# A language-model layer on one core: front reordered, and batch 1's stage with its row of maxima sent sooner

## The reference

```
h = einsum('bsd,bsde->bse', base[ids], rule_transform[token_rules[ids]])
h = h + attention(layernorm(h))    # softmax(q k^T / 8) over 512 keys, 8 heads
h = h + experts(layernorm(h))      # top 2 of 8, relu, softmax of the two gates
```

## Time and profile before

| | |
|---|---|
| three runs | 608.01, 612.52, 615.87 us; median 612.52 |
| profiled execution | 610.8 us, its span 608.8 us, granted clock 0.93 |
| busy in the span | PE 495.7 (81%), DVE 411.8 (68%), ACT 287.2 (47%), POOL 229.1 (38%) |
| chain that ended last | PE 55%, DVE 18%, POOL 9%, issue 8%, DMA 4%, ACT 4%, SP's queue 2% |

### The profile page before, as it was taken

One profiled execution on the slowest core, in us unless ns is written; L12 is line 12 of the kernel. 1 busy time (PEld: TensorE's weight loads), 2 busy tenths in 40 slices (PEclk: granted clock), 3 DMA queues, 4 the chain that ended last, 5 costly groups with the idle time before them and its releaser, 6 DMA issues.

```text
span 608.8 us, 9495 instructions
## 1 busy us (share of the span) xinstructions
PE 495.7 (81%) x2764; PEld 270.0 (44%) x2764; DVE 411.8 (68%) x1003; ACT 287.2 (47%) x581; POOL 229.1 (38%) x375
## 2 busy tenths in 40 slices
PE   0168404878777888999999999999999999999985
PEld 0036302444442334445544544554454445576663
DVE  5634288883126756888868968986984876755477
ACT  0205101037663535465565565555566545547673
POOL 5765356462425200431352254032322313181542
PEclk9999665579998997999999999999999999999988
DMA  8825210919620171532330431134042200000000
GB/s 237 316 65 168 62 35 28 210 57 232 195 79 18 35 171 36 123 74 63 82 76 2 104 90 34 30 90 101 2 104 63 52 2 11 1 10 2 11 2 17
DMA packets 21792, 47.05 MB, mean 77 GB/s; under 512 B 6249, under 2 KB 11577, under 8 KB 21681
## 3 DMA queue, kind: packets, MB, share of 16 engines
q1 hardware_dynamic: 15408, 32.23, 21.9%
q0 software_dynamic: 4752, 8.20, 4.5%
q10 hardware_dynamic: 1584, 6.03, 3.0%
HBM read 9.97 MB, written 11.01 MB: 34 GB/s over the span
## 4 chain that ended last, share of the span: by engine, by line
PE 55%; DVE 18%; POOL 9%; issue 8%; DMA 4%; ACT 4%; SPq 2%; DVEq 0%; ACTq 0%; POOLq 0%
PE bank L1304 15%; PE bank L1290 10%; PE bank L1266 7%; POOL ctxT L522 5%; PE bank L1214 4%; PE bank L1236 4%; DVE mx L1009 4%; DMA ctxT<-in_table,ids 2%; PE bank L1208 2%; PE bank L1209 2%; DVE r_sb L1067 2%; POOL r_sb L595 2%; POOL emb_sorted L532 1%; PE bank L1315 1%; PE bank L1249 1%
## 5 line engine op out<-in xcount | busy, mean ns | idle before, releaser
L1009 DVE TENSOR_REDUCE mx<-bank 128x1 f32<-128x512 f32 x256 | 170.7, 687 | 79.0 <-PE bank L1290 72.8
L595 POOL TENSOR_TENSOR r_sb<-r_sb 128x256 f32<-128x256 f32 x174 | 90.9, 523 | 248.9 <-DVE r_sb L1085 168.5
L675 ACT ACTIVATE prob<-bank 128x512 f32<-128x512 f32 x256 | 138.8, 597 | 68.7 <-PE bank L1266 56.3
L1304 PE MATMUL bank<-prob,xa 128*64 128x512 f32 x448 | 123.5, 630 | 0.0
L1290 PE MATMUL bank<-ks,qs 96*128 96x512 f32 x240 | 111.4, 467 | 13.9 <-DVE mx L1009 13.8
L1290 PEld LDWEIGHTS bank<-ks,qs 96*128 96x128 f32 x240 | 46.2, 193 | 121.8 <-issue 103.4
L1266 PE MATMUL bank<-qs,ks 97*128 97x512 f32 x224 | 77.3, 427 | 0.0
L742 ACT ACTIVATE r_sb<-bank,stay 128x512 f32<-128x512 f32 x56 | 37.1, 687 | 44.9 <-PE bank L1209 44.6
L1266 PEld LDWEIGHTS bank<-qs,ks 97*128 97x128 f32 x224 | 38.6, 194 | 15.3 <-issue 10.5
L522 POOL DMA_INDIRECT ctxT<-in_table,ids x32 | 33.2, 1036 | 22.5 <-DMA ctxT<-in_table,ids 9.6
L532 POOL DMA_INDIRECT emb_sorted<-ctxT,pos x32 | 32.3, 1009 | 20.4 <-DMA emb_sorted<-ctxT,pos 12.2
(11 more groups left out here) (173 smaller groups left out, 696.2 us busy)
## 6 DMA issues: line engine op xcount, KB each, us to landing
qs<-qk_h SPq DMA_DIRECT2D x64, 128.0 KB, 2.5
ks<-qk_h SPq DMA_DIRECT2D x56, 128.0 KB, 2.5
qs<-qk_l SPq DMA_DIRECT2D x32, 128.0 KB, 2.5
ks<-qk_l SPq DMA_DIRECT2D x28, 128.0 KB, 2.4
emb_sorted<-front ACTq DMA_DIRECT2D x4, 608.0 KB, 9.7
y_sorted<-y_out POOLq DMA_DIRECT2D x19, 128.0 KB, 2.4
e_in<-emb_sorted POOLq DMA_DIRECT2D x9, 256.0 KB, 4.0
emb_sorted<-front ACTq DMA_DIRECT2D x3, 640.0 KB, 9.7
```

Source lines behind the costliest of these rows:

```text
L595: nc.gpsimd.tensor_tensor(a[:, at:at + width], src[:, 0:width], src[:, width:2 * width], ALU.add).then_inc(S["pool_chain"], 1)
L675: nc.scalar.activation(prob[:, step % NPROB, u % 2, :], bank[u % NST][:], ACT.Exp, scale=SC).then_inc(S["exp_done"], 1)
L1009: V.tensor_reduce(mx[:, u // 16, at_:at_ + 1], score_bank(n)[:], AX.X, ALU.max).then_inc(S["mx_done"], 1)
L1304: last = M(bank[5][64 * hh:64 * hh + 64, :], xa[:, b % XAR, ut, :], prob[:, step, hh, :], start=(ut == 0), stop=(ut == J - 1))
```

## The change

- Front, DVE: within the 15 groups only quarter 2 is looked at (after groups 5 to 8). Quarter 3's look and `starts(1)` follow the loop. PE counts quarter 3 after the last group has been evicted. The slots of quarters 1, 2 and 3 all come after the norm of batch 0, moved on at steps 1, 2, 5 (twice) and 7 of stage -2, and the rest at (-2,9); quarters 2 and 3 are one double run with one set of small operations.
- Front, POOL: the memset of `xa` goes ahead of the last 14 fetches; `values(0)` stands behind quarter 1's scatter instead of behind that of quarters 1 and 2.
- `tile_rules(1)` and `rule_row(1)` move from (-2,9) to (-1,15).
- Rule groups start at (0,2) instead of (0,3). Batch 1: norm (0,0), xT (0,2), proj (0,2) and (0,3), before (-1,12), (-1,15), (0,0) and (0,1). Batch 2: norm (0,10), xT (0,12), proj (0,13) and (0,14), before (0,11), (0,14) and (0,15). Batch 3: xT (1,8), proj (1,9) to (1,12), before (1,4) and (1,5) to (1,8). rt of batch 0: (1,8), before (1,6).
- SP: in b = 1, max_row(1,1) comes first; srow, stack(2,2) and stack(2,3) follow. stack(2,2) is no longer sent in b = 0.

```diff
-        R_AT = [(0, 3 + g // 4) for g in range(20)]
+        R_AT = [(0, 2 + g // 4) for g in range(20)]
-            return {1: (-1, 15), 2: (0, 14)}.get(nb, (nb - 2, XT))
+            return {1: (0, 2), 2: (0, 12), 3: (1, 8)}.get(nb, (nb - 2, XT))
-            return {1: ((0, 0), (0, 0), (0, 1), (0, 1)), 2: ((0, 15), (0, 15), (0, 15), (0, 15))}.get(
+            return {1: ((0, 2), (0, 2), (0, 3), (0, 3)), 2: ((0, 13), (0, 13), (0, 14), (0, 14)),
+                    3: ((1, 9), (1, 10), (1, 11), (1, 12))}.get(
                 nb, [(nb - 2, k) for k in PROJ])
-            if k == RT and 0 <= b - 1 < B:
+            if k == (RT if b != 1 else 8) and 0 <= b - 1 < B:
             for b in range(-2, B):
+                if b == 1:
+                    max_row(1, 1)
                 if 0 <= b - 1 < LAST:
 ...
+                if b == 1:
+                    stack(2, 2)
                 if 0 <= b + 1 < B:
                     stack(b + 1, 3)
-                if 0 <= b < B:
+                if 0 <= b < B and b != 1:
                     max_row(b, 1)
 ...
-                if 0 <= b + 2 < B:
+                if 0 <= b + 2 < B and b != 0:
                     stack(b + 2, 2)
 ...
             place(0, range(FIRST))
+            nc.gpsimd.memset(xa[:], 1.0).then_inc(S["xa_set"], 1)
             for c in range(FIRST + 10, NC):
 ...
-            nc.gpsimd.memset(xa[:], 1.0).then_inc(S["xa_set"], 1)
 ...
-            place(1, range(FIRST, FIRST + 2 * QC))
+            place(1, range(FIRST, FIRST + QC))
             values(0)
-            place(1, range(FIRST + 2 * QC, NC))
+            place(1, range(FIRST + QC, NC))
 ...
-            def slots(i, q):
+            def slots(i, q, parts=1):
+                c0, c1 = q * QC, (q + parts) * QC
 ...
+                for p in range(parts):
+                    at_ = c0 - lo + p * QC
+                    link(V.tensor_tensor(sel[:], oh[:, at_:at_ + QC, :], key.unsqueeze(1).to_broadcast([128, QC, NR]), ALU.mult))
+                    yield
+                    link(V.tensor_reduce(slot_f[:, p * QC:(p + 1) * QC], sel[:], AX.X, ALU.add))
+                    yield
 ...
-            later = chain(look(1, 2), look(1, 3))
+            later = look(1, 2)
 ...
-                if 5 <= g < 9 or g >= 11:
+                if 5 <= g < 9:
                     next(later, None)
-            run(later)
+            run(look(1, 3))
             starts(1)
-            run(slots(1, 1))
-            run(slots(1, 2))
 ...
-            N_AT = {1: (-1, 12), 2: (0, 11), 3: (0, 15)}
+            N_AT = {1: (0, 0), 2: (0, 10), 3: (0, 15)}
 ...
-                    later = slots(1, 3)
+                    later = chain(slots(1, 1), slots(1, 2, 2))
 ...
                     if (b, k) == (-2, 9):
                         run(later)
+                    if (b, k) == (-1, 15):
                         tile_rules(1)
-                    if b == -2 and k in (1, 2, 5, 6, 7, 8):
+                    for _ in range({1: 1, 2: 1, 5: 2, 7: 1}.get(k, 0) if b == -2 else 0):
                         next(later, None)
 ...
-                    for _ in range(4 if b == -1 else 3 if b == 0 else 3 if b == LAST else 1):
+                    for _ in range((4 if k < 3 else 3) if b == 0 else 3 if b == LAST else 1):
 ...
-                if g in (8, 11, 13):
-                    count(1, (8, 11, 13).index(g) + 1)
+                if g in (8, 11):
+                    count(1, (8, 11).index(g) + 1)
             pe.wait_ge(S["y_ok"], NG[0])
+            count(1, 3)
 ...
-                    if (b, k) == (-2, 9):
+                    if (b, k) == (-1, 15):
                         rule_row(1)
```

More of the change, by code:

```diff
@@ L170, in lm_tower_kernel @@
             trule = tb("trule", [128, 1])
-            slot_f = tb("slot_f", [128, QC])
-            slot_i = tb("slot_i", [128, 11, QC], I32)
+            slot_f = tb("slot_f", [128, 2 * QC])
+            slot_i = tb("slot_i", [128, 11, 2 * QC], I32)
         with ExitStack() as part:
@@ L529, in place @@
                         pool.wait_ge(S["scattered_1"], 16 * (c - FIRST))
-                    if c % QC == 0:
+                    if c in (0, QC, 2 * QC):
                         pool.wait_ge(S["pos_ok"], c // QC + 1)
@@ L823, in starts @@
                 link(V.scalar_tensor_tensor(key, first, float(B * T), cum, ALU.mult, ALU.add))
-            def slots(i, q):
-                c0, c1 = q * QC, (q + 1) * QC
+            def slots(i, q, parts=1):
+                c0, c1 = q * QC, (q + parts) * QC
                 lo = SPAN[i][0]
[L829 to L834, removed]
+                both, nth, ahead, at_in, past, gap, tile_, hi, mid, low, two = (slot_i[:, j, 0:c1 - c0] for j in range(11))
+                for p in range(parts):
[4 more added lines that the diff above has]
+                    yield
+                link(V.tensor_tensor(both, slot_f[:, 0:c1 - c0], rank[:, c0:c1], ALU.add))
                 link(V.tensor_scalar(nth, both, SHIFT, (B * T >> SHIFT) - 1, ALU.logical_shift_right, ALU.bitwise_and))
```

## The result

The changed kernel takes 625.62 us (median of four runs, 623.97 to 626.20) against 612.09 (four runs, 608.01 to 615.87): ratio 1.0209, interval 1.0161 to 1.0257. It is slower; whether by more than 2% the interval leaves open. The profiled execution took 623.97 us, span 622.0, against 610.8 and 608.8: 13.2 us more, where I forecast 6.05 (median 617, range 605 to 626).

A forecast was written before the change was run, and what follows sets the result against it. TensorE, 81% busy, was taken as dense except in the first third, where waits break its beat at four places. Terms -2.3 + 3.5 + 2.15 - 1.0 - 3.6 + 7.3 = +6.05 on 610.8 gave 616.9, forecast 617, range 605 to 626.

The forecast's parts named there:

- Front: Up to the first rule group: gathers and norm come sooner, rules start at 137.8 instead of 141.0, 3.2 us sooner.
- So the scatter starts where it started before: POOL's scatter: waits ten us for slots now behind the norm, starts at 90.9 and ends at 133.8, no change.
- holds two more projections (0.9): Rule section: starts 3.2 us sooner but holds two more projections costing 0.9, together -2.3 us.
- I take +3.5: Rule section: a cold start after some 8 us idle slows four groups and one step, +3.5 us, bounds 0 and 16.6.
- The extra step and the wait for the gather of batch 2: Behind the rules: same wait, one more step left behind it, +2.15 us; batch 2's projections two by two, -1.0 us.
- (1,5) to (1,12): Stage 1: the 8.3 us lost at (1,6) become 4.7, with a wait of 2.7 at (1,10): -3.6 us, bounds -5.6 to 0.
- (1,15): Stage 1: new wait of 4.5 us for the row of maxima behind two stacks, +7.3 us with clock loss, bounds +4.5 and +8.
- Rival 1: Scatter: faster for the change, first rule group at 132.6, clock kept: -2.7 us, 608 us, chance 0.2.
- Rival 2: Rule section: stays at the lower clock from start to end, 16.6 in place of 3.5: 630 us, chance 0.1.
- Rival 3: Stage 1: ACT, stopped at (1,9), also holds the exponentials; the whole 8.3 us remain: +9.7, 620.5 us, chance 0.12.
- rival 4: Stage 1: stalls at (1,6) and (1,15) both vanish and rival 1 holds: -14.7 us, 596 us, chance 0.05.
- Nothing later takes it back: Stages from b=2 on keep their beat, so a gain or loss up to there moves the end by the same amount.

The follow-up runs named there:

- experiment 5: The changed kernel unaltered, run again on another chip: 633.14 us, ratio 1.0286 to the kernel before.
- experiment 9: The kernel of experiment 1 with slot run 1 put back in front of the norm of batch 0: 603.14 us, ratio 0.9855.
- experiment 6: The changed kernel with eight extra matmuls of 384 columns, results unused, ahead of the first rule group: 632.53 us, ratio 1.0265.
- experiment 7: The changed kernel with batch 1 (norm, x, projections) back where it was, rule groups still from (0,2): 622.07 us, ratio 1.0156.
- experiment 2: The changed kernel without its stage 1 part (batch 3, SP's order and rt as before): 627.47 us, ratio 1.0227.
- experiment 4: The changed kernel with max_row(2,0) moved ahead of stack(3,0) and stack(3,1) on SP's queue: 624.42 us, ratio 1.0153.
- experiment 12: The changed kernel with the edits of experiment 4 and experiment 9, and stack(2,2) sent in b = 0: 604.56 us, ratio 0.9898.
- experiment 11: The kernel of experiment 10 with the norm of batch 2 at (0,12) instead of (0,11): 593.81 us, ratio 0.9691.
- experiment 8: The kernel of experiment 3 with the edit of experiment 4 and stack(2,2) sent in b = 0 again: 604.38 us, ratio 0.9813.
- experiment 1: The changed kernel's front alone, with rule groups, batches 1 to 3 and SP's order as in the kernel before: 618.48 us, ratio 1.0101.
- experiment 10: The edits of experiment 8 and experiment 9 together: 601.92 us, ratio 0.9802 to the kernel before.
- experiment 3: The kernel before with the change's stage 1 part alone (batch 3's xT and projections, rt, SP's order): 618.46 us, ratio 1.0102.

## Why the prediction was right or wrong

- **The result as a whole.** The time, 625.62, lies 0.4 us inside the range's end of 626 and outside the 611 to 623 that I gave my own forecast; "slower" had a chance of 0.11. In experiment 5, on another chip, all four runs of the same kernel (631.44 to 635.55) lie above the range. That the range held is in part luck.
- **Front: right, within 2.7 us.** Forecast against measured: gathers 70.8 and 69.13, norm 78 and 75.74, maxima 99.5 and 96.80, start of the scatter 90.9 and 89.13, e_in load 133.8 and 131.88, first rule group 137.8 and 135.23. "So the scatter starts where it started before" holds, and experiment 9 shows that it was the order of norm and slots that held it. The start of the gathers was right by luck: I had the loop end at 68.3 and the stores 2.5 us behind it, but it ended at 65.0, and the fetches, which I had left out, ended the wait. TensorE was idle for 4.99 us ahead of the rules, where I had some 8.
- **Rules: the step that failed is the term of the section, "holds two more projections (0.9)" and "I take +3.5".** That makes a section of 42.4 us; it took 49.2, 6.8 more (2.6 of it made good by the sooner start). By sets, the 11.2 us over the kernel before are 5.85 in the first (12.38 against 6.53), 3.1 in the second (11.76 against 8.67) and 2.25 in the third (11.19 against 8.93); the rest is as long as before.
  - The first set takes 8.60 us when it runs warm (experiment 6). So the cold start cost 3.8 us in this execution, close to the 3.5, though only 1.4 in experiment 5 and 1.8 in experiment 7. The two projections, with PE's wait of 0.94 for their qk_l, cost the other 2.1, not 0.9.
  - The 5.35 us of the second and third set I had put at nothing. I had not asked when batch 1's first stack must be there: its scores want it at (0,4), and the last projection now stands in (0,3), before in (0,1). By the chain of waits above these scores start at 156.15, 20.9 us behind the first turn; before, the tile behind the second set started 13.4 behind it. So 7.5 of the 11.2 us, the cold start among them, are set by the path from the rules' start over projections and remainder to the stack. The other 3.7 are slow clock behind it.
  - In all traces with the changed placement the stack ends a wait, 19 to 22 us after the first turn, with slow matmuls behind it: 0.73 us in the first profile, 2.89, 2.96, 1.34, 3.79 and 1.91 in experiments 2, 4, 5, 6 and 12. With batch 1 early it does so once, for 0.38 us (experiment 9).
  - In the first profile the clock had fallen just before that wait, at 153.14. What let it fall is not settled: the small waits there (0.94 for qk_l at 147.61, 0.71 and 0.85 for ACT) stand in experiment 12 too, at full clock, and in experiment 11, with no stack wait, it fell behind one of 1.05 us for ACT (an apply at 143.89 takes 1.12 us).
- **The extra step and the wait for the gather of batch 2: right.** +2.15 and -1.0 were forecast behind the section, together +1.15; measured +1.5 (from +5.4 to +6.9). The wait itself is 3.79 us, before 3.94.
- **(1,5) to (1,12): place and releaser right, size not.** The wait at (1,10) is 2.38 us where I had 2.7, ended by qk_l. The net is -1.9 instead of -3.6.
- **(1,15): right.** A wait of 5.50 us ended by the row's transfer, forecast 4.5; from (1,12) to (2,0) it costs 8.2, forecast 7.3. Experiment 4 takes it away by the queue order alone.
- **Sum.** 6.05 + 4.2 (section) + 0.35 + 1.7 + 0.9 = 13.2. Of the error of 7.15 us, 4.2 are one term.
- **The rivals.** Rival 1 (the scatter is faster) did not come: it took 42.75 us instead of 42.85. Its two long waits moved forward with the stacks, to 98.54 (3.84 us) and 106.90 (3.16). Rival 2 had the right consequence in part. The Trainium skill ("TensorE: Matmul & The Clock Gate", section "A second HAM failure mode: psum-queue depth-cycling") says that small idles between groups can keep the clock switching between its two levels. It does not say that it stays low, as rival 2 had it. The trace agrees with the switching: applies of 1.12 us up to 140.16, of 0.69 at 148 to 151, of 1.12 from 153.14 and of 0.69 from 171.16 on. The section was thus not cold from start to end, and experiment 7, with idles of 0.58 and 0.95 us between its groups at 151.90 and 153.88, stayed at 1.00. Rival 3, the whole 8.3 us staying, did not come: 1.9 were won, about half way between it and the forecast. The time of rival 4 (596) was reached by experiment 11 (593.81) alone, with two edits of order that the change lacked and with batches 1 and 2 and the rule groups where they had been.
- **What I did not know.** The 617 assumed that part 0's loop takes what it took before. In the changed kernel it ended at 65.0 in one execution and at 76.8 in another, and the time followed (medians 625.6 and 633.1). "Nothing later takes it back" also failed once, in the profiled execution of experiment 8.

## What to carry to other kernels

When a queue issues in program order and waits for a transfer to land, ask of each small transfer on which the next step waits what stands ahead of it: twelve stack issues ahead of one row of maxima cost 8.2 us, and moving that row in front of them won it back. When work is moved under an idle stretch, follow its last consumer and not only the engine that does it; the projections of batch 1 inside the rule groups looked cheap, and their stack came late. And a front that is relieved of one engine's wait gains only if the next queue's producer moves too: here the slots ahead of the norm, not behind it.

## What the runs showed that I had not expected

- **Part 0's loop has two speeds.** Gathers start at 69 to 71 us in five profiled executions of the reordered front (the changed kernel, experiments 7, 9, 11, 12) and at 77 to 80 in six (experiments 1, 2, 4, 5, 6, 10). These groups lie on different chips, and all of one chip agree. In the loops of the slower ones DVE has waits of 1.1 to 3.5 us whose releaser the trace doesn't name, as before 62.58 and 70.40 above; the quick ones have none. The kernel before doesn't show it, since the loop ended behind the look at the last quarter in any case: its gathers start at 80.44, and with that front unchanged, in experiments 3 and 8, at 80.46 and 80.06. The cause is open; no run was made for it.
- **The clock after a long idle stretch comes back soon, but not evenly.** After 8.11 us idle (experiment 7) the applies at 142.32 take 1.12 us, and those from 149.34 on 0.69; the clock is back 6 us after the first turn. After 4.99 us idle (first profile) it takes some 10.
- **The clock can be low in dense work.** In experiment 8's profile it fell behind a wait of 1.21 us (until 480.55) and stayed at 0.50 from 482.78 to 499.20, though TensorE was busy all the time; in the kernel before the same steps run at 1.00. What started and ended it is open. A loss of 7.8 us in one execution is as large as most effects here, so a difference of a few us between two single executions decides little by itself.
